# Four attention and expert layers on one core: tokens sorted by expert into tiles of 128 slots

## The reference

```
x = x + attention_l(layernorm(x), context)     # 16 heads of 8, 1024 queries, 6404 keys
x = x + experts_l(layernorm(x))                # 8 experts, the best 2 for each token
```

```
L0: softmax weights, an expert takes at most 512 tokens; h = silu(x A) * (x G) of 192 features, y = h C
L1: two rounds of z = z + experts(rmsnorm(z)); h of 256 features, weights that sum to 1
L2: h = gelu(x U) of 512 features, softmax weights
L3: h = silu(x A + a) * (x G + g) of 256 features, y = h C + c, weights that sum to 1
```

## Time and profile before

| | us |
|---|---|
| median of 3 runs | 4366.84 |
| lowest, highest | 4354.51, 4367.82 |
| the profiled execution | 4359.73 |
| its span | 4358.0 |
| mean granted clock of TensorE | 0.968 |

### The profile page before, as it was taken

The page is one execution under the profiler, slowest core; times in us unless marked ns, Lnnn a source line. Parts: engine busy times, 40 slices in busy tenths (PEclk is TensorE's granted clock), DMA queues, the critical chain, the costliest instruction groups (busy, mean ns, idle before and its releaser), DMA issues.

```text
span 4358.0 us, 71738 instructions
## 1 busy us (share of the span) xinstructions
PE 4055.6 (93%) x27834; PEld 1089.2 (25%) x27834; DVE 2893.0 (66%) x6026; ACT 3834.7 (88%) x4271; POOL 587.2 (13%) x545
## 2 busy tenths in 40 slices
PE   7899999999999999999999999899999999999997
PEld 2122222222222222222222222223122232222223
DVE  6889888788987788777603232111686778988833
ACT  3699998989999899888998888889999888999994
POOL 3000002220022211323221101000000000011100
PEclk7699999999999999999999999999999999999998
DMA  5211001000001110010001111011000000000000
GB/s 147 70 28 36 25 25 31 21 21 18 13 20 39 37 36 26 26 31 22 27 23 42 47 35 53 24 35 37 14 15 20 18 24 17 13 16 18 11 14 22
DMA packets 112813, 130.33 MB, mean 30 GB/s; under 512 B 27912, under 2 KB 75024, under 8 KB 112400
## 3 DMA queue, kind: packets, MB, share of 16 engines
q1 hardware_dynamic: 111744, 125.27, 10.3%
q10 hardware_dynamic: 720, 0.40, 0.0%
HBM read 102.24 MB, written 23.34 MB: 29 GB/s over the span
## 4 chain that ended last, share of the span: by engine, by line
PE 61%; ACT 17%; DVE 14%; issue 3%; POOL 0%; DMA 0%; ACTq 0%; SPq 0%; POOLq 0%; DVEq 0%
PE av L1243 25%; ACT prob L1399 13%; PE scores L1233 12%; DVE mpart L1507 10%; PE side L1265 8%; PE scores L1340 6%; PE side L1353 4%; DVE above L1511 3%; PE side L1340 1%; PE scores L1256 1%; ACT above L1409 1%; PE side L1233 1%; PE scores L1380 1%; PE scores L1376 1%; ACT ag L1461 0%
## 5 line engine op out<-in xcount | busy, mean ns | idle before, releaser
L1399 ACT ACTIVATE prob<-scores 128x1024 f32<-128x1024 f32 x2999 | 2905.0, 1032 | 189.9 <-PE scores L1233 98.3
L1507 DVE TENSOR_REDUCE mpart<-side 128x1 f32<-128x512 f32 (+1 forms) x3456 | 2075.9, 655 | 391.6 <-PE side L1265 381.5
L1243 PE MATMUL av<-prob,VB 128*9 128x512 f32 x6528 | 871.6, 607 | 0.6 <-ACT prob L1399 0.5
L1243 PE MATMUL av<-prob,VA 128*9 128x512 f32 x6528 | 863.5, 601 | 1.7 <-ACT oS L1419 0.8
L1265 PE MATMUL side<-KA,QP 32*128 32x512 f16 (+1 forms) x2112 | 596.5, 393 | 66.9 <-DVE mpart L1507 40.7
L1233 PE MATMUL scores<-QP,KA 32*128 32x512 f16 x2998 | 579.9, 389 | 38.9 <-ACT prob L1399 23.1
L1265 PE MATMUL side<-KB,QP 32*128 32x512 f16 (+1 forms) x2112 | 551.5, 381 | 60.0 <-DVE mpart L1507 32.9
L1233 PE MATMUL scores<-QP,KB 32*128 32x512 f16 x3000 | 575.9, 387 | 30.5 <-ACT prob L1399 16.5
L1511 DVE CUSTOM_DVE_ANT_0 above<-side,above 128x512 f32<-128x512 f32 x768 | 503.5, 686 | 116.9 <-PE side L1265 100.6
L1409 ACT ACTIVATE above<-scores 128x1024 f32<-128x1024 f32 x384 | 395.4, 1030 | 61.7 <-DVE mpart L1511 41.9
L1233 PEld LDWEIGHTS scores<-QP,KB 32*128 32x128 f16 x3000 | 138.7, 91 | 776.3 <-ACT prob L1399 642.4
(11 more groups left out here) (196 smaller groups left out, 2316.9 us busy)
## 6 DMA issues: line engine op xcount, KB each, us to landing
KA<-kstacks SPq DMA_DIRECT2D x384, 48.0 KB
KB<-kstacks SPq DMA_DIRECT2D x384, 48.0 KB
Fin<-in_Fin SPq DMA_DIRECT2D x64, 256.0 KB, 2.6
kstacks<-hi SPq DMA_DIRECT2D x100, 128.0 KB, 2.4
ctxc<-in_ctxT SPq DMA_DIRECT2D x36, 256.0 KB, 3.0
hT<-in_mask SPq DMA_DIRECT2D x16, 400.2 KB, 3.5
kstacks<-lo SPq DMA_DIRECT2D x50, 128.0 KB, 2.5
Fout<-in_Fout SPq DMA_DIRECT2D x48, 128.0 KB, 2.7
```

Of the source, the lines that this page charges most:

```text
L1243: last = pe.matmul(AV[ROWS * h:ROWS * h + VC, :], V[l % 2][:, kt, g * HG + h, :], prob[:, (e + h // 2) % RING, (h % 2) * QB:(h % 2) * QB + ...
L1399: act.activation(prob[:, e % RING, :], pair.rearrange("p a b -> p (a b)"), ACT.Exp if softmax(l) else ACT.Sigmoid, scale=SCALE).then_inc(s ...
L1507: dve.tensor_reduce(part, bank, AX.X, ALU.max).then_inc(sem["red"], 1)
```

## The change

A pass no longer runs every expert on every token. The 1024 choices of the 512 tokens are sorted by expert into tiles of 128 slots, each tile for one expert; the parts of eight experts, each rounded up, need at most 15 tiles, and 15 are always computed. The steps of a pass now are:

1. `logit`, the router as before, then at once `routec` and `count` (prefix sums by matmul with a triangle of ones, and a third small matmul for totals) in all layers; `slota` to `slotd` (14 small operations on VectorE) give each choice its slot and each tile its expert.
2. `scat`: eight indirect DMAs from GpSimd write the tokens (once for each choice) to the slots of a buffer in DRAM; `xload`: four plain DMAs by SyncE bring it back, four tiles each.
3. `gT`, `gTc`: each tile is transposed on TensorE, four to a bank, and copied by ScalarE.
4. For each tile, `win` and `wout`: an indirect DMA each from GpSimd fetches the 128 rows of the tile's expert's weights, into one ring of six. `up` is four matmuls of 128 columns into one bank; `agc` copies all of it (512 wide) to SBUF, on ScalarE in layers 0 and 1 except unit 3, on VectorE elsewhere, in layer 3 with the bias; `tanh` is 256 wide, from SBUF; `gatea` and `gateb` are 256 wide, always on VectorE. `down` is two (layer 2: four) matmuls of 128 columns, `yc` a copy of 128 columns on VectorE. Layer 2: `upc`, then a Gelu of 512 a tile in batches of three, with the `down` four tiles behind.
5. `yput`: four plain DMAs write the results to DRAM; `yget`: eight indirect DMAs from GpSimd bring each token's two results; `ysum`: eight operations on VectorE in all add them.

Here is the core of the diff (waits and repeated edits left out):

```diff
-W_RING = 3
+W_RING = 6
+W_LEN = 516
 H_RING = 4
-BIAS_AT = 2
+GELUS = 3
+HID_RING = 2 * GELUS
+ST = 2 * QB // P + E - 1
+SLOTS = ST * P
+FOURS = [range(i, min(i + 4, ST)) for i in range(0, ST, 4)]
...
-WIDE = (15, 8), (22, KT - 4)
+WIDE = (15, 8), (20, 0)
...
 def pass_steps(u, lp):
...
+    n = behind(l)
+    by = "DVE" if by_dve(u, lp) or l == 3 else "ACT"
+    fetch = deque(Step("POOL", w, k) for w, k in fetches_of(u, lp))
+    out = [Step("PE", "logit", (u, lp))]
+    out += [Step("DVE", what, (u, lp)) for what in ("routea", "routeb", "routee", "routef", "routeg", "routec", "routeh")]
+    out += [Step("PE", "count", (u, lp))]
+    out += [Step("DVE", what, (u, lp)) for what in ("slota", "slotb", "slotc", "slotd")]
+    out += [Step("ACT", "rexp", (u, lp))]
+    out += [Step("DVE", what, (u, lp)) for what in ("routej", "routek", "routel", "routed")]
+    out += [Step("POOL", "scat", (u, lp, c)) for c in range(2)]
+    out += [Step("SP", "xload", (u, lp, i)) for i in range(len(FOURS))]
+    out += [fetch.popleft() for i in range(W_RING)]
...
+    out += turned(0)
+    for j in range(ST + n):
+        if j < ST:
+            if j % 4 == 2 and j // 4 + 1 < len(FOURS):
+                out += turned(j // 4 + 1)
+            out.append(Step("PE", "up", (u, lp, j)))
+            if f["gated"]:
+                out += [Step(by, "agc", (u, lp, j)), Step("ACT", "tanh", (u, lp, j))]
+            else:
+                out.append(Step(by, "upc", (u, lp, j)))
+            out += next_fetch()
+        if j >= n:
+            k = j - n
+            out += [Step("PE", "down", (u, lp, k)), Step("DVE", "yc", (u, lp, k))]
+            out += next_fetch()
+            if k % 4 == 3 or k == ST - 1:
+                out.append(Step("SP", "yput", (u, lp, k // 4)))
+        if j < ST:
+            if f["gated"]:
+                out += [Step("DVE", what, (u, lp, j)) for what in ("gatea", "gateb")]
+            elif j % GELUS == GELUS - 1 or j == ST - 1:
+                out += [Step("ACT", "gelu", (u, lp, k)) for k in range(j - j % GELUS, j + 1)]
+    out += [Step("POOL", "yget", (u, lp, c)) for c in range(2)]
+    out += [Step("DVE", "ysum", (u, lp, c)) for c in range(2)]
...
-    PE=dict(av=0.853, up=0.858, down=0.858, ...
+    PE=dict(av=0.853, up=0.89, down=0.45, gT=0.39, count=0.5, ...
+    POOL=dict(gatea=0.65, gateb=1.45, ksplit=1.82, fill=0.56, zcopy=0.56, var=0.16, rstd=1.0, square=1.0, scale=1.0, center=1.0, win=1.3, wout=1.3,
+              scat=5.2, yget=5.2),
...
                 elif s.what == "up":
+                    for i in range(4):
+                        last = pe.matmul(bank[0:fs, i * P:(i + 1) * P], W[:, w, i * fs:(i + 1) * fs], xgT[:, j * P:(j + 1) * P], start=True, stop=True)
...
                 elif s.what == "down":
+                    for c in range(nk):
+                        last = pe.matmul(bank[:, 0:D], h[:, c * P:(c + 1) * P], W[0:fs, w, c * D:(c + 1) * D], start=c == 0, stop=c == nk - 1)
...
+                elif s.what == "scat":
+                    for t in range(QT):
+                        to = bass.IndirectOffsetOnAxis(ap=slot[:, QT * c + t:QT * c + t + 1], axis=0)
+                        pool.indirect_dma_start(xslot, to, xn[:, t, :], None).then_inc(sem["d_scat"], 16)
+                elif s.what in ("win", "wout"):
+                    own.wait_ge(*o.sem("slotd", u, lp))
+                    if fetch_before(s.what, s.key):
+                        used, k = fetch_before(s.what, s.key)
+                        own.wait_ge(*o.sem(used, *k))
+                    at = bass.IndirectOffsetOnAxis(ap=widx[:, j:j + 1], axis=0)
+                    pool.indirect_dma_start(W[:, w, 0:n], None, A[f"{s.what}{unit(u)[0]}"], at).then_inc(sem[f"d_w{w}"], 16)
+                elif s.what == "yget":
+                    own.wait_ge(*o.sem("yput", u, lp, len(FOURS) - 1))
+                    for t in range(QT):
+                        at = bass.IndirectOffsetOnAxis(ap=slot[:, QT * c + t:QT * c + t + 1], axis=0)
+                        pool.indirect_dma_start(y12[:, QT * c + t, :], None, yslot, at).then_inc(sem[f"d_yget{c}"], 16)
```

More of the change, by code:

```diff
@@ L181, in by_dve, with behind, passes, pass_before @@
     return u in (3, 4, 7)
-def hidden(k):
-    return k % 3
+def behind(l):
+    return 1 if FFN[l]["gated"] else GELUS + 1
+def passes(u):
+    return [(u, lp) for lp in range(FFN[u // 2]["loops"])]
+def pass_before(u, lp):
+    order = [x for v in range(8) for x in passes(v)]
+    i = order.index((u, lp))
+    return order[i - 1] if i else None
+def fetches_of(u, lp):
+    n = behind(unit(u)[0])
+    return [(w, (u, lp, k)) for j in range(ST + n) for w, k in (("win", j), ("wout", j - n)) if 0 <= k < ST]
+FETCHES = [x for u in range(8) for v in passes(u) for x in fetches_of(*v)]
+def weights_used(what, key):
+    return ("down" if what == "wout" else "agc" if unit(key[0])[0] == 3 else "up"), key
+def fetch_before(what, key):
+    i = FETCHES.index((what, key))
+    return weights_used(*FETCHES[i - W_RING]) if i >= W_RING else None
 Step = namedtuple("Step", "eng what key home", defaults=(None,))
@@ L281, in __init__ @@
                 used[i] = [last_use(s.what, s.key)]
[L282 to L285, removed]
+            elif s.what in SIDE:
+                self.bank[s.what, s.key], self.before_it[s.what, s.key] = idle.pop(0)
+                held[last_use(s.what, s.key)] = s.what, s.key
             if (s.what, s.key) in held:
@@ L403, in pass_steps @@
+    assert not fetch
+    out += [Step("POOL", "yget", (u, lp, c)) for c in range(2)]
+    out += [Step("DVE", "ysum", (u, lp, c)) for c in range(2)]
     return out
@@ L721, in other @@
     def other(self, s, mode, start):
-        hold = HOLD["PE"].get(s.what, USUAL["PE"])
+        hold = HOLD["PE"].get(s.what, USUAL["PE"]) * (2 if s.what == "down" and s.key[0] in (4, 5) else 1)
         self.mode, self.t, self.until = mode, start, start + hold
@@ L732, in take_bank @@
             self.holds[last_use(s.what, s.key)] = "pair", i
-        elif s.what != "down" or s.key[-1] == 0:
+        else:
             i, t = self.side.pop(0)
-            self.holds[last_use(s.what, s.key[:-1] if s.what == "down" else s.key)] = "side", i
+            self.holds[last_use(s.what, s.key)] = "side", i
     def bank_free(self, s):
@@ L740, in bank_free @@
             return t is not None and t <= self.t
-        if s.what == "down" and s.key[-1]:
-            return True
         return bool(self.side) and self.side[0][1] <= self.t and not self.widening
@@ L865, in choose @@
                 s = self.placed_at(self.heads["PE"][i][0])
-                if s.home != "pair" and (s.what != "down" or s.key[-1] == 0):
+                if s.home != "pair":
                     reserved = 1
```

599 lines of the change are left out of this document (305 added, 294 removed).

## The result

The changed kernel takes 4222.6 us in the median of its runs (4221.3 to 4226.3), the kernel before 4362.0 beside it (4354.5 to 4367.8): ratio 0.9683, 95% interval [0.9663, 0.9702]. The profiled execution took 4226.3 us (span 4224.0), the one of before 4359.7. So 133 us are gone; from the execution of before 145 had been forecast, and a median of 4218.

The account below looks back on a forecast made before the run. No single engine was taken to bound the kernel: TensorE, ScalarE and VectorE hand each other buffers in fixed order. 4359.7 - 170 + 25 = 4215, stated as 4218 us; range 4150 to 4325, own range 4180 to 4260 (chance 0.48).

Parts of the forecast that it names:

- TensorE's saving: Nine expert passes beside attention: matmul work falls from 403 to 219 us, saving 184 us.
- ScalarE's saving: Nine expert passes: copies, tanh, Gelus and table loads fall from 206 to 126 us, saving 80 us.
- VectorE: Layers with maxima: VectorE gains 77 us of work, priced at a third, so 27 us off the saving.
- Price of 0.74: Expert phases beside attention: 0.74 us of time for each microsecond of TensorE or ScalarE work, from a 527 us pool.
- Sum beside attention: Attention phases: 0.74 x (184 + 80) = 195, less 27 for VectorE, 168, called 170 us saved.
- The indirect DMAs: GpSimd: 1.3 us each, 46 a pass; GpSimd stays under 25% and the fetches' landing is covered.
- The tail: Tenth pass, alone behind attention: grows by 25 us, as routing, scatters and GpSimd's 30 fetches are uncovered.
- Rival 1: Side work beside attention: TensorE alone sets its price; saves 216 - 25, giving 4168 down to 4150 us; chance 0.2.
- Rival 2: Attention phases: ScalarE and VectorE bind once TensorE is relieved; saves 80 - 25, giving 4305 us; chance 0.18.
- Rival 3: Scatter and gather chains come later than planned; gain of 145 gone at 2.3 us per DMA, 4520 at 3; chance 0.11.
- The rule of the shared port: VectorE's 210 gates and GpSimd's SBUF reads exclude each other: 10 us of VectorE, some 4 on the end, 4222 us.
- What would show it: Expert phases 120 to 130 us, up and down about 190, ACT's idle in them halved, GpSimd near 20%, tail near 104.

Follow-up runs that it names:

- One kernel, two chips: The changed kernel with its 300 weight fetches as plain SyncE DMAs from fixed experts: 4301.5 us (ratio 0.9878) in the first group, 4219.1 us (0.9676) in the third.

## Why the prediction held, step by step

- **TensorE's saving.** 184 us forecast, 186.0 measured beside attention (3861.2 to 3675.2). The size is shown, but two omissions lie in it and cancel: the rows of up and down fell by 263 us, those of transposes and counts rose by 32, which leaves 231; the other matmuls, the same in number, then take 45 us more, with 63 us more of half clock, in which every matmul takes longer. The forecast had no term for the clock.
- **ScalarE's saving.** 80 forecast, 87.4 measured. Shown.
- **VectorE.** Forecast +77 us in the groups with maxima. Summed over their five stretches it is 1993.9 before and 2015.3 after, +21, but this hides the term: the lines that find maxima (1507 and 1511, then 1552 and 1556) take 36 us less in these groups, since the order moved 40 reductions and 10 of the others into unit 4's. All else that VectorE does in the five takes 135 us before and 208 after, +73. So the work was forecast rightly. Its price was low: a third, against the 0.42 to 0.46 that the runs show, each with the doubt told above. 73 x 0.45 is some 33 us for the 27 that were taken off.
- **Price of 0.74.** Added to the changed kernel, TensorE's work costs 0.98 and ScalarE's 0.67. Taken away from the kernel before, both together gave back less: with 33 us for VectorE (158.7 + 33) / (186.0 + 87.4) = 0.70; with 10, if what VectorE lost in the groups of units 3 and 4 gave time back at the same price, 0.62. That two prices at one point are not what the road to it pays is shown; the reason is not.
- **Sum beside attention.** -170 forecast, -158.7 measured, that is 11 us too much. The savings were 9 us too small, worth 7 us of time. VectorE's price was 6 us too low, and the 0.74, with which the measured savings would be 202, was 10 to 34 us too high. TensorE's term is right only with what the clock took.
- **The indirect DMAs.** 1.3 us forecast, 1.25 measured. The rows left it open between 0.33 and 1.49 or more, so a value this near is partly luck. GpSimd is at 17% (forecast near 20). Beside attention the fetches cost nothing that can be seen: without 270 of them (and with an order planned for that) the stretch is 2.9 us longer, not shorter.
- **The tail.** +25 forecast, +27.7 measured, for a partly wrong reason. GpSimd does issue its 30 fetches nearly without pause (4153.8 to 4193.9), but with plain fetches the tail is only 7.3 us shorter, and still 21 longer than before. What makes it long is the chain: routing, eight scatters, reload, 15 tiles, store, eight gathers. Behind the fetches the next limit is at hand: with plain ones a tile starts about every 2 us, which VectorE's four operations for it fill (0.68, 0.29, 0.42 and 0.42, and the time between them), and the two fetches take 2.5. The terms of 2 us for landing and 3 for the reload had no row; from the last scatter's end to the first transpose 4.9 us passed.
- **Rival 1** (TensorE alone, 4168) is half right: its price at the margin is 0.98. But ScalarE's is 0.67 and VectorE's 0.4 to 0.5, so it isn't alone.
- **Rival 2** (ScalarE and VectorE bind, 4305) would have every group gain little. Only unit 4's gained nothing, and there ScalarE's work grew and maxima and half clock came in from elsewhere, so it doesn't speak for the rival.
- **Rival 3** (chains of DMAs late) did not come, by a margin of 4.2 us in the mean: beyond that, one chain of each pass is as exposed as it says, as the run with ten more operations shows, and the slower clock comes on top. With indirect DMAs at 2.3 us the scatters would have cost 9 x (8 - 4.2) = 34 us of waits beside attention, some 45 with the clock, by that run's 67.7 for 51.6 (an estimate). The rival's 145 left out the slack and counted the chain of gathers as well, which no run lengthened.
- **The rule of the shared port.** The Trainium skill ("SBUF — State Buffer", shared port pair) would have made the gates longer, by 10 us in all. Beside attention the 210 gates take 95.1 us, 7 more than at the 0.42 that one alone takes. The trace agrees with the rule, in fewer cases than were taken: of the 240 gates ten met GpSimd's ordinary work, for the 17 of 210 that the estimate has; seven of them took 502 to 1857 ns, three no longer than alone, some 3.5 us in all above ten others. Some 4 us more lie in the gates of line 1755 that ran beside indirect DMAs (463 ns in the mean, 415 without GpSimd). The longest stands here:

```profile
L1761 DVE TENSOR_TENSOR gates<-gates x120: 404/423/1857, 713.4 to 4196.9; 128x256 f32<-128x256 f32 x90, 96x256 f32<-96x256 f32 x30
```

- **What would show it.** Of the 28 phases behind the first four, 8 are still over 130 us (16 before), the longest 149.8: "120 to 130" is right in the mean only. Up and down stand at 264 us of records, not 190, since the estimate was a pace and the records overlap (before 528 for 403: the halving is right). ScalarE's idle time more than halved in the phase of 157.2 us (23.0 to 8.9), but over all it went only from 367 to 296.

## What to carry to other kernels

Where three engines alternate in a fixed order, price a saving per engine by adding work to each in turn with the order held still. The 0.98, 0.67 and 0.46 here say that gates belong on the idle engine, and with them there (+177 us of it, and an order planned anew) the kernel took 21 us less: this part of the change seems to have worked against the rest. Before a chain of DMAs is trusted to be hidden, read the slack from its landing to its first consumer, for beyond it each microsecond was paid in full here, once per pass, and the lower clock behind the wait came on top. When work is summed by stretch, count what the new order moved across the stretch's ends before a term is called wrong. And when a variant comes out far from all theories, look first for waits that no other trace has, and run the changed kernel itself beside its variants.

## What the runs showed of the hardware that was not expected

- One kernel, two chips, 4301.5 and 4219.1 us, while the kernel before took 4357.6 and 4361.4 beside it. In the longer case all three engines have waits on nothing visible, 14 us in all on TensorE and up to 7.3 us at once on ScalarE, and the half clock beside attention goes from 192 to 262 us. So 14 us of such waits went with 72 us of time beside attention. Why that chip and not the kernel before stays open.
- The granted clock fell where TensorE had short pauses: of 29 stretches at 1.2 GHz beside attention in the changed kernel 23 last 3.4 or 6.8 us, and the longest pause shortly before one is 0.2 to 3.0 us (the longer ones behind Gelus with their table loads of 1.28 us). But ten of the 25 that begin beside attention in the kernel before follow pauses of at most 0.22 us, so the pause alone doesn't tell. The half clock did not follow TensorE's load either: with 120 us of matmuls added back it is 204 us (201 and 189 in the two profiles without), with more work on ScalarE 175, with less on VectorE 158, in the kernel before 137. What sets it stays open.
- An indirect DMA of 128 rows costs GpSimd 0.95 to 0.98 us whether a row has 512 bytes or some 2000 (979 and 946 ns the scatters and gathers of 512, 955 the fetches of `win` of 1536 to 2064, in the mean), plus 0.30 us to the next.
